# Perceiver attention reordered: K in its own layout, two heads on halves of the array, batches written out

## Chip, core and metric

The kernel runs on one core of a Trainium2 chip. The time is that of one execution on the device in microseconds (us), the median of several runs; fewer is better.

## The reference

Two layers, each a gated cross attention and a gated mixture of experts, on x of 8 x 100 x 512 with a context of 8 x 722 x 512, all fp32. The change is in the first step, a perceiver attention in which the 100 rows of x are the latents and the context gives the keys:

```
def _L0_xattn_ref(x, latents, mask, ...):        # x: context 8x722x512, latents: 8x100x512
    xn = layernorm(x, ln_x_g, ln_x_b)
    ln = layernorm(latents, ln_l_g, ln_l_b)
    q = ln @ Wq                                  # 512 -> 16 heads of 64
    kv = concatenate((xn, ln), axis=1) @ Wkv     # 822 keys a batch, 512 -> 2 x 1024
    k, v = split(kv, 2, axis=-1)
    sim = einsum('bhid,bhjd->bhij', heads(q) * 64 ** -0.5, heads(k))
    sim = where(mask_full, sim, max_neg)
    attn = softmax(sim, axis=-1)
    out = einsum('bhij,bhjd->bhid', attn, heads(v)) -> 8 x 100 x 1024
    return layernorm(out @ Wout, ln_o_g, ln_o_b)
x = x + tanh(g_xattn[0]) * _L0_xattn_ref(ctx, layernorm(x), mask, ...)
```

Behind it come the first mixture (4 experts), a strided attention and the second mixture (8 experts). They are not touched.

## The kernel before

Each step is a stage of its own with a block of instructions for each engine; the engines run in their own written order and meet at semaphores. The stage of the change is `perceiver_attention`.

At the start it loads the weights `wkv` in eight pieces and splits each in two fp32r parts, hi (a rounded copy, ScalarE) and lo (the difference, VectorE). It then works batch by batch, eight of them, in a hardware loop of seven turns and a last turn written out. A batch has 822 keys (722 context rows and 100 latents, in seven tiles of up to 128 rows) and 16 heads in eight pairs (hp = 0 to 7).

- **Normalising**: VectorE's `moments` and `normalise` in the middle of the batch before, GpSimd's `scale` (two operations a tile) behind it.
- **prepare**: TensorE transposes a normalised tile (L402) into one of the two banks of `kv_ps`, ScalarE copies hi (L281; for the latents also `lat_t`), VectorE subtracts lo (L581).
- **queries**: 32 fp32 matmuls (L411) into `s_ps`; ScalarE and VectorE write `q_hi` and `q_lo` in eight pieces each (L290, L596), each head's copy on both halves of the partitions.
- **keys(hp, part)**: K of a pair of heads in two parts of 512 and 310 columns, each four steps of three matmuls (`three`, L388 to L390: hi x hi, and the two cross terms). ScalarE copies hi of each head (64 partitions) into `k_two`, VectorE puts lo on the other 64 partitions (L305, L603), so that one matmul over 128 rows contracts q with hi and lo of k at once.
- **values(half, t)**: V of four pairs for a tile of keys, the same three terms, 12 matmuls of 512 columns (also L388 to L390), copied by ScalarE (L297). A half's seven tiles stand in one run: the first half at the start of the batch, the second behind pair 4.
- **scores(hp, x)**: for head x of the pair two passes, `q_hi` and `q_lo`, over two parts (L451, L452), into `s_ps`, which holds one head.
- **maximum** (VectorE, L613, adds the mask and keeps the row maximum), **exponent** (ScalarE, L315), **divide** (VectorE, L618 and L619).
- **transposes(hp, x)**: seven of 100 x 128 (L465) into the two banks of `t_ps`, four and three; ScalarE copies head 0 (L311), VectorE head 1 (L625), both called `move_t`.
- **attend(hp)**: 14 matmuls (L476), the two heads on halves of the output's partitions, that is of the array's columns; VectorE's `move_o` copies the result (L630).
- **finish**: the projection with `wout` (eight fp32 matmuls, L485, into the bank `w_ps`), the output's layernorm and the residual (L634 to L645).

TensorE's order in pairs 1 to 7 is, for x in 0, 1: transposes(hp-1, x), scores(hp, x), keys(hp+1, x); then attend(hp-1). The eight banks of 512 fp32 columns are: `kv_ps` 2, `s_ps` 2, `t_ps` 2, `o_ps` 1, `w_ps` 1.

## Time and profile before

| | us |
|---|---|
| median of 3 runs | 2489.97 (2474.49 to 2490.97) |
| profiled execution | 2482.1 |
| its span | 2479.9 |
| perceiver stage in it | 0 to 1,137 |

The profile is of one execution. PE is TensorE's matmul, PEld its weight loads, DVE VectorE, ACT ScalarE, POOL GpSimd. Busy times of PE overlap each other, since matmuls are pipelined and their ends are modelled: what a matmul costs is read from the distance between the starts of two that follow each other. In a timeline a bracket gives the idle time before a row and what ended it. PEclk is the clock that TensorE was granted, as a share of 2.4 GHz.

### The profile page before, as it was taken

Reading aid. Unit: us, or ns where it says so; the run is one execution under the profiler, and the core shown is the slowest. Engines: PE = TensorE matmul, PEld = TensorE weight load, DVE = VectorE, ACT = ScalarE, POOL = GpSimd, SP = SyncE. Lnnn points to the kernel's source line nnn. Section 1 sums busy time; section 2 is a strip of 40 time slices with the busy share of each in tenths; the row PEclk is TensorE's granted clock in tenths of the full one; section 3 lists DMA queues with packets and bytes.
Section 4 is the critical chain, followed back from the end, with each engine's and each line's share of the span. In section 5 each row is a group of like instructions: output and inputs, shape, how many; then the busy total and the mean of one; then the engine's idle time right before and its main releaser. Section 6 shows DMA issues by size and latency. Waiting matters only on the chain. (4 is left out here: it accounts for less than half of the span.)

```text
span 2479.9 us, 39705 instructions
## 1 busy us (share of the span) xinstructions
PE 2062.0 (83%) x12984; PEld 1706.0 (69%) x12984; DVE 1242.9 (50%) x2517; ACT 975.6 (39%) x2047; POOL 599.4 (24%) x547
## 2 busy tenths in 40 slices
PE   2899999999999999994499999999568627888783
PEld 2777878787878777772377777777466517787682
DVE  4484847576665657453333333333045354445444
ACT  2453445444444444442333333332343234444440
POOL 4030302012030303000333333331111023455443
PEclk9999999999999999996699999999786758899896
DMA  6001010100001010003533333331860164444436
GB/s 218 2 1 36 1 36 1 37 1 17 21 1 36 1 36 1 8 1 123 189 98 98 101 102 102 94 96 64 246 172 0 41 235 160 133 123 135 144 119 174
DMA packets 105987, 198.68 MB, mean 80 GB/s; under 512 B 13978, under 2 KB 14778, under 8 KB 105850
## 3 DMA queue, kind: packets, MB, share of 16 engines
q1 hardware_dynamic: 98896, 182.10, 23.1%
q0 software_dynamic: 6144, 13.13, 2.0%
q8 instruction: 85, 1.39, 0.2%
q10 hardware_dynamic: 810, 1.64, 0.2%
q14 instruction: 52, 0.43, 0.1%
HBM read 164.83 MB, written 31.98 MB: 79 GB/s over the span
## 5 line engine op out<-in xcount | busy, mean ns | idle before, releaser
L249 POOL TENSOR_TENSOR a_rows<-a_rows,a_gain_x 128x512 f32<-128x512 f32 (+1 forms) x48 | 71.2, 1484 | 803.2 <-DVE a_rows L570 803.2
L715 PE MATMUL f_banks<-f_wab_hi,f_x_hi 128*128 x448 | 189.1, 422 | 17.2 <-DVE f_wab_lo L1286 13.7
L305 ACT ACTIVATE a_k_two<-a_kv_ps 64x512 fp32r<-64x512 f32 (+1 forms) x256 | 130.1, 508 | 170.9 <-PE a_kv_ps L390 167.6
L715 PE MATMUL m_banks<-m_wab_hi,m_x_hi 128*128 x512 | 164.8, 322 | 31.2 <-DVE m_wab_lo L1286 27.8
L603 DVE TENSOR_TENSOR a_k_two<-a_kv_ps,a_k_two 64x512 fp32r<-64x512 f32 (+1 forms) x256 | 149.4, 584 | 78.3 <-ACT a_k_two L305 72.9
L388 PE MATMUL a_kv_ps<-a_wkv_hi,a_kvin_hi 128*128 128x512 f32 (+1 forms) x448 | 179.4, 401 | 9.4 <-DVE a_k_two L603 9.4
L388 PE MATMUL a_kv_ps<-a_kvin_hi,a_wkv_hi 128*128 128x512 f32 (+1 forms) x512 | 183.7, 359 | 0.6
L1316 DVE TENSOR_TENSOR f_h_sb<-f_s_sb,f_banks 128x256 f32<-128x256 f32 x112 | 47.2, 421 | 272.0 <-ACT f_s_sb L1082 272.0
L390 PE MATMUL a_kv_ps<-a_kvin_hi,a_wkv_lo 128*128 128x512 f32 (+1 forms) x512 | 179.8, 351 | 0.0
L389 PE MATMUL a_kv_ps<-a_kvin_lo,a_wkv_hi 128*128 128x512 f32 (+1 forms) x512 | 178.7, 349 | 0.0
L716 PE MATMUL f_banks<-f_wab_lo,f_x_hi 128*128 x448 | 178.6, 399 | 0.0
L717 PE MATMUL f_banks<-f_wab_hi,f_x_lo 128*128 x448 | 178.2, 398 | 0.0
L389 PE MATMUL a_kv_ps<-a_wkv_lo,a_kvin_hi 128*128 128x512 f32 (+1 forms) x448 | 177.4, 396 | 0.0
L390 PE MATMUL a_kv_ps<-a_wkv_hi,a_kvin_lo 128*128 128x512 f32 (+1 forms) x448 | 176.9, 395 | 0.0
L315 ACT ACTIVATE a_probs<-a_probs,a_neg_max 100x822 f32<-100x822 f32 x128 | 125.8, 983 | 109.3 <-DVE a_neg_max L613 108.3
L716 PE MATMUL m_banks<-m_wab_lo,m_x_hi 128*128 x512 | 153.0, 299 | 0.0
L717 PE MATMUL m_banks<-m_wab_hi,m_x_lo 128*128 x512 | 152.9, 299 | 0.0
L613 DVE CUSTOM_DVE_ANT_0 a_probs<-a_s_ps,a_mask_add 100x822 f32<-100x822 f32 x128 | 129.6, 1012 | 45.1 <-PE a_s_ps L452 42.9
L297 ACT ACTIVATE a_v_sb<-a_kv_ps 128x512 f32<-128x512 f32 (+1 forms) x112 | 66.8, 596 | 216.6 <-PE a_kv_ps L390 216.6
L1082 ACT ACTIVATE f_s_sb<-f_banks 128x256 f32<-128x256 f32 x112 | 43.0, 384 | 253.3 <-PE f_banks L717 253.3
L1016 POOL TENSOR_TENSOR f_wy_lo<-f_raw,f_wy_hi 128x512 fp32r<-128x512 f32 x64 | 83.0, 1296 | 233.8 <-ACT f_wy_hi L1060 233.8
L715 PEld LDWEIGHTS m_banks<-m_wab_hi,m_x_hi 128*128 128x128 f32 x512 | 106.3, 208 | 34.5 <-issue 34.5
(349 smaller groups left out, 5156.3 us busy)
## 6 DMA issues: line engine op xcount, KB each, us to landing
f_raw<-f_pieces SPq DMA_DIRECT2D x192, 256.0 KB, 2.7
m_raw<-m_pieces SPq DMA_DIRECT2D x192, 256.0 KB, 2.8
a_rows<-ctx SPq DMA_DIRECT2D x8, 1280.0 KB
g_rows<-ctx SPq DMA_DIRECT2D x8, 1280.0 KB, 10.0
...
```

What stands on the lines that cost most here:

```text
L249: own.link(nc.gpsimd.tensor_tensor(row, row, g[0:n, :], ALU.mult))
L305: nc.scalar.activation(k_two[halves[x], hp % 2, x, c:c + n], kv_ps[halves[x], c:c + n], ACT.Copy).then_inc(k_hi_done, 1)
L315: nc.scalar.activation(probs[0:M, x, 0:KEYS], probs[0:M, x, 0:KEYS], ACT.Exp, scale=-1.0, bias=neg_max[0:M, x:x + 1], accum_out=row_sum[0: ...
L388: nc.tensor.matmul(out, hi_l, hi_r, start=first, stop=False)
L389: nc.tensor.matmul(out, hi_l, lo_r, start=False, stop=False)
L390: return nc.tensor.matmul(out, lo_l, hi_r, start=False, stop=last)
L603: ins = nc.vector.tensor_tensor(k_two[halves[1 - x], hp % 2, x, c:c + n], kv_ps[halves[x], c:c + n], k_two[halves[x], hp % 2, x, c:c + n]. ...
L613: nc.vector.tensor_tensor_reduce(out=probs[0:M, x, 0:KEYS], in0=s_ps[0:M, 0:KEYS], in1=mask_add[0:M, :], scale=-1.0, scalar=3.0e38, op0=AL ...
L715: nc.tensor.matmul(out, left_hi, right_hi, start=start, stop=False)
L716: nc.tensor.matmul(out, left_hi, right_lo, start=False, stop=False)
L717: return nc.tensor.matmul(out, left_lo, right_hi, start=False, stop=stop)
L1016: nc.gpsimd.tensor_tensor(split_dst(wab_lo, wy_lo, c), raw[:, n % RING, :], split_dst(wab_hi, wy_hi, c).bitcast(F32), ALU.subtract).then_i ...
```

## The change

- **K**: one `k_hi` and one `k_lo` in the layout in which K leaves PSUM (two heads on 128 partitions), one copy and one subtraction a part, one buffer instead of two. `q_hi` and `q_lo` likewise, in two pieces each instead of eight.
- **Scores**: both heads in one call. `s_ps` has four banks, two for each head. Each head takes three passes (hi x hi, hi x lo, lo x hi) over its 64 partitions; the heads alternate matmul by matmul.
- **V**: two buffers (`v_sb` by half). The 14 tiles are spread over pairs 0 to 5 by FILL = 4, 3, 2, 2, 2, 1, behind the pair's other work.
- **Transposes**: one bank `t_ps`. Four tiles, copied by ScalarE, then three, copied by VectorE, for each head. The bank `w_ps` is gone: queries and projection go through `o_ps` like attend.
- **Order**: TensorE runs scores(n), attend(n-2), then the transposes of n-1 in four rounds between halves of keys(n+1), then values. The projection of a batch stands in pair 1 of the next, its layernorm in pairs 2 and 4. The latents' tile is prepared first (ORDER). All of a batch's `prepare`, the next batch's first keys and its queries stand in pair 7.
- **Start**: eight staging buffers for `wkv`; K's halves of the weights come and are split first, V's halves after the first queries.
- **Batches** are written out, eight times the code instead of a loop; bank use is counted per bank (`kv_free`, `o_free`).

The diff, cut to what the text speaks of:

```diff
-        k_two = sb("k_two", [P, 2, 2, KEYS], F32R)
-        v_sb = sb("v_sb", [P, KT, HALF])
-        q_hi = sb("q_hi", [P, PAIRS, 2, M], F32R)
-        q_lo = sb("q_lo", [P, PAIRS, 2, M], F32R)
+        k_hi = sb("k_hi", [P, KEYS], F32R)
+        k_lo = sb("k_lo", [P, KEYS], F32R)
+        v_sb = sb("v_sb", [P, 2, KT, HALF])
+        q_hi = sb("q_hi", [P, PAIRS, M], F32R)
+        q_lo = sb("q_lo", [P, PAIRS, M], F32R)
...
-        kv_ps = ps("kv_ps", [P, 2 * BANK])
-        s_ps = ps("s_ps", [P, 2 * BANK])
-        t_ps = ps("t_ps", [P, 2 * BANK])
+        stage = [wout_sb[:, :, :].rearrange("p k n -> p (k n)")[:, SW * n:SW * n + SW] for n in range(4)]
+        stage += [v_sb[:, :, :, :].rearrange("p h t n -> p (h t n)")[:, SW * n:SW * n + SW] for n in range(4)]
+
+        kv_ps = ps("kv_ps", [P, 2, BANK])
+        s_ps = ps("s_ps", [P, 2, 2 * BANK])
+        t_ps = ps("t_ps", [P, BANK])
         o_ps = ps("o_ps", [P, BANK])
-        w_ps = ps("w_ps", [P, BANK])
...
+        FILL = [4, 3, 2, 2, 2, 1, 0, 0]
...
-                if n >= STAGE:
-                    sp.wait_ge(w_lo_done, 1 + n - STAGE + 1)
-                sp.dma_start(stage[n % STAGE], wkv[P * (n // 2):P * (n // 2 + 1), SW * (n % 2):SW * (n % 2 + 1)]).then_inc(w_loaded[n % STAGE], 16)
-                if n == STAGE - 1:
-                    sp.dma_start(wq_sb[:, :, :], wq.rearrange("(k p) n -> p k n", p=P)).then_inc(pq_loaded, 16)
-            sp.wait_ge(w_lo_done, 1 + 2 * KD)
+                k, half = n % KD, n // KD
+                sp.dma_start(stage[n], wkv[P * k:P * k + P, SW * half:SW * half + SW]).then_inc(w_loaded[n], 16)
+                if n == KD - 1:
+                    sp.dma_start(wq_sb[:, :, :], wq.rearrange("(k p) n -> p k n", p=P)).then_inc(wq_loaded, 16)
...
-            def keys(i, hp, part):
-                c, n = PART[part]
-                act.wait_ge(k_ready, 1 + 2 * PAIRS * i + 2 * hp + part + 1)
-
-                act.wait_ge(s_ready, 1 + 2 * PAIRS * i + (2 * hp - 2 if hp >= 2 else 0))
-                for x in range(2):
-                    nc.scalar.activation(k_two[halves[x], hp % 2, x, c:c + n], kv_ps[halves[x], c:c + n], ACT.Copy).then_inc(k_hi_done, 1)
...
+            def keys(n, part):
+                c, w = PART[part]
+                act.wait_ge(k_ready, 2 * n + part + 1)
+                if n:
+                    act.wait_ge(s_ready, 2 * n)
+                nc.scalar.activation(k_hi[:, c:c + w], kv_bank("k", n, part)[:, 0:w], ACT.Copy).then_inc(k_hi_done, 1)
...
+                    if hp < PAIRS - 1 or i + 1 == B:
+                        if n:
+                            move_t(n - 1, 0)
+                        if hp < PAIRS - 1:
+                            keys(n + 1, 0)
+                        if n:
+                            move_t(n - 1, 1)
+                        exponent(n, 0)
+                        if hp < PAIRS - 1:
+                            keys(n + 1, 1)
...
-            def scores(i, hp, x):
-                pe.wait_ge(k_lo_done, 1 + 2 * PAIRS * i + 2 * hp + 2)
-                pe.wait_ge(q_lo_done, 1 + i + 1)
-                pe.wait_ge(max_done, 1 + 2 * PAIRS * i + 2 * hp + x)
-                for c, n in PART:
-                    k = k_two[:, hp % 2, x, c:c + n]
-                    nc.tensor.matmul(s_ps[0:M, c:c + n], q_hi[:, hp, x, :], k, start=True, stop=False)
-                    ins = nc.tensor.matmul(s_ps[0:M, c:c + n], q_lo[:, hp, x, :], k, start=False, stop=True)
-                ins.then_inc(s_ready, 1)
...
+            def scores(n):
+                i, hp = divmod(n, PAIRS)
+                if hp % QP == 0:
+                    pe.wait_ge(o_free, o_use["q", i, hp // QP] + 1)
+                wait_read(pe, ("k", n, 0), ("k", n, 1))
+                if n:
+                    pe.wait_ge(max_done, 2 * n)
+                for c, w in PART:
+                    for step, (q, k) in enumerate(((q_hi, k_hi), (q_hi, k_lo), (q_lo, k_hi))):
+                        for x in range(2):
+                            ins = nc.tensor.matmul(s_ps[0:M, x, c:c + w], q[halves[x], hp, :], k[halves[x], c:c + w],
+                                                   start=(step == 0), stop=(step == 2))
+                            if c and step == 2:
+                                ins.then_inc(s_ready, 1)
...
+            for i in range(B):
+                for hp in range(PAIRS):
+                    n = PAIRS * i + hp
+                    scores(n)
+                    if n >= 2:
+                        attend(n - 2)
+                    if hp < PAIRS - 1:
+                        if n:
+                            transposes(n - 1, 0, 0)
+                        keys(n + 1, 0, ALL[:KD // 2])
+                        if n:
+                            transposes(n - 1, 0, 1)
+                        keys(n + 1, 0, ALL[KD // 2:])
+                        if n:
+                            transposes(n - 1, 1, 0)
+                        keys(n + 1, 1, ALL)
+                        if n:
+                            transposes(n - 1, 1, 1)
+                    elif i + 1 < B:
+                        prepare(i + 1, ORDER[0])
+                        prepare(i + 1, ORDER[1])
+                        transposes(n - 1, 0, 0)
+                        prepare(i + 1, ORDER[2])
+                        transposes(n - 1, 0, 1)
+                        prepare(i + 1, ORDER[3])
+                        transposes(n - 1, 1, 0)
+                        prepare(i + 1, ORDER[4])
+                        queries(i + 1, 0)
+                        transposes(n - 1, 1, 1)
+                        prepare(i + 1, ORDER[5])
+                        prepare(i + 1, ORDER[6])
+                        keys(n + 1, 0, ALL)
+                        keys(n + 1, 1, ALL)
+                        queries(i + 1, 1)
+                    else:
+                        for x in range(2):
+                            for r in range(2):
+                                transposes(n - 1, x, r)
+                    if hp == 0 and i == 0:
+                        pe.wait_ge(w_lo_done, 2 * KD)
+                    for v in range(V_FROM[hp], V_FROM[hp] + FILL[hp]):
+                        if hp == 1 and i and v == V_FROM[hp] + 1:
+                            finish(i - 1)
+                        values(i, v)
...
+                    if n >= 2:
+                        move_o(n - 2)
+                    if hp < PAIRS - 1 or i + 1 == B:
+                        if n:
+                            move_t(n - 1, 0)
+                        maximum(n, 0)
+                        if hp < PAIRS - 1:
+                            keys(n + 1, 0)
+                        divide(n, 0)
+                        if n:
+                            move_t(n - 1, 1)
+                        maximum(n, 1)
+                        if hp < PAIRS - 1:
+                            keys(n + 1, 1)
+                        divide(n, 1)
+                    else:
...
+                    if hp == 2 and i:
+                        ins = project(i - 1)
+                        if i + 1 == B:
+                            ins.then_inc(var_done, 1)
+                    if hp == 4:
+                        wait_std()
+                        first, end = (0 if i + 1 < B else OUT), (NT + 1 if i else NT)
+                        own.link(nc.vector.reciprocal(rstd[:, first:end], std[:, first:end]))
+                        if i + 1 < B:
+                            again_latent()
+                        if i:
+                            finish(i - 1)
+                    if hp == 5 and i + 1 < B:
+                        last_latent()
+                        normalise_rows(range(0, 3))
+                    if hp == 6 and i + 1 < B:
+                        normalise_rows(range(3, CT))
...
```

## Rows read from the trace of the kernel before

**Rows 1.** The page: busy us of each engine, share of the span, instructions.

```profile
PE 2062.0 (83%) x12984; PEld 1706.0 (69%) x12984; DVE 1242.9 (50%) x2517; ACT 975.6 (39%) x2047; POOL 599.4 (24%) x547
```

**Rows 2.** Windows: the perceiver stage; PE, PEld, DVE, ACT, POOL busy, PEclk, DMA.

```profile
0.00:1137.00 1137.00, 1032.75 (x6944) 838.81 (x6944) 698.87 (x1360) 500.36 (x945) 163.50 (x123) 0.99 0.08 25
```

**Rows 3.** PE's timeline (start us, us): projections of two batches, queries between them.

```profile
596.63 0.59 PE L485 MATMUL a_w_ps<-a_wout_sb,a_out_t 128*100 128x512 f32 x1
...
722.96 0.35 PE L411 MATMUL a_s_ps<-a_lat_t,a_wq_sb 128*128 128x100 f32 x1
...
730.18 0.59 PE L485 MATMUL a_w_ps<-a_wout_sb,a_out_t 128*100 128x512 f32 x1
```

**Rows 4.** PE's timeline: attend, transposes, scores of one head.

```profile
652.95 1.42 PE L476 MATMUL a_o_ps<-a_probs_t,a_v_sb 128*64 128x100 f32 x28
654.30 0.82 PE L465 MATMUL a_t_ps<-a_ident,a_probs 100*128 100x100 f32 x7
654.90 0.45 PE L451 MATMUL a_s_ps<-a_k_two,a_q_hi 128*100 128x512 f32 x1
655.19 0.39 PE L452 MATMUL a_s_ps<-a_k_two,a_q_lo 128*100 128x512 f32 x1
655.42 0.30 PE L451 MATMUL a_s_ps<-a_k_two,a_q_hi 128*100 128x310 f32 x1
655.56 0.31 PE L452 MATMUL a_s_ps<-a_k_two,a_q_lo 128*100 128x310 f32 x1
```

**Rows 5.** PE's timeline at the edge of a batch.

```profile
716.60 0.64 PE L476 MATMUL a_o_ps<-a_probs_t,a_v_sb 128*64 128x100 f32 x9 [1.22 <-issue]
```

**Rows 6.** Groups by form, 0 to 1,140 us; then the timeline of DVE and ACT.

```profile
L603 DVE TENSOR_TENSOR a_k_two<-a_kv_ps,a_k_two 64x310 fp32r<-64x310 f32 x128 | 61.3, 479 | 3.2
...
L305 ACT ACTIVATE a_k_two<-a_kv_ps 64x310 fp32r<-64x310 f32 x128 | 54.2, 424 | 91.8 <-PE a_kv_ps L390 90.2
...
L581 DVE TENSOR_TENSOR a_kvin_lo<-a_kv_ps,a_kvin_hi 128x512 fp32r<-128x512 f32 x40 | 26.1, 682 | 1.5 <-ACT a_kvin_hi L281 1.5
...
L281 ACT ACTIVATE a_kvin_hi<-a_kv_ps 128x512 fp32r<-128x512 f32 x40 | 22.4, 598 | 22.3 <-PE a_kv_ps L402 22.3
...
656.12 1.00 DVE L613 CUSTOM_DVE_ANT_0 a_probs<-a_s_ps,a_mask_add 100x822 f32<-100x822 f32 x1
...
657.16 0.98 ACT L315 ACTIVATE a_probs<-a_probs,a_neg_max 100x822 f32<-100x822 f32 x1 [1.30 <-DVE a_neg_max L613]
...
658.27 0.16 DVE L618 RECIPROCAL a_row_inv<-a_row_sum 100x1 f32<-100x1 f32 x1 [1.14 <-ACT a_probs L315]
658.47 0.65 DVE L619 TENSOR_SCALAR a_probs<-a_probs,a_row_inv 100x822 f32<-100x822 f32 x1
...
659.03 0.95 DVE L625 COPY a_probs_t<-a_t_ps 128x400 f32<-128x400 f32 x2
```

**Rows 7.** DVE's timeline while GpSimd scales rows.

```profile
567.86 2.15 DVE L619 TENSOR_SCALAR a_probs<-a_probs,a_row_inv 100x822 f32<-100x822 f32 x1
```

**Rows 8.** Timeline: the stage's last prepare and first queries; its last write.

```profile
49.84 0.93 PE L402 MATMUL a_kv_ps<-a_ident,a_lat 100*128 100x100 f32 x4 [1.76 <-POOL a_lat L250]
...
51.80 9.54 PE L411 MATMUL a_s_ps<-a_lat_t,a_wq_sb 128*128 128x100 f32 x64 [1.03 <-issue]
...
1135.54 0.75 DVE L645 SCALAR_TENSOR_TENSOR a_tail<-a_tail,a_tanh_g,a_res 100x512 f32<-100x512 f32 x1
```

**Rows 9.** PE's timeline after two waits; the window behind the first.

```profile
71.64 0.79 PE L388 MATMUL a_kv_ps<-a_wkv_hi,a_kvin_hi 128*128 128x512 f32 x1 [5.76 <-DVE a_k_two L603]
72.23 0.63 PE L389 MATMUL a_kv_ps<-a_wkv_lo,a_kvin_hi 128*128 128x512 f32 x1
72.66 0.63 PE L390 MATMUL a_kv_ps<-a_wkv_hi,a_kvin_lo 128*128 128x512 f32 x1
...
71.60:75.60 4.00, 3.96 (x9) 3.14 (x10) 1.49 (x3) 0.00 (x0) 0.00 (x0) 0.50 0.13 18
...
1115.14 2.60 PE L476 MATMUL a_o_ps<-a_probs_t,a_v_sb 128*64 128x100 f32 x28 [1.84 <-issue]
```

732 lines of the change are left out of this document (354 added, 378 removed).

## The prediction, made before the changed kernel was run

> **What bounds the kernel now.** I read the page's busy times first, then the table of stages. Over the kernel TensorE (PE) is busy 83%; in the perceiver stage, 1,137 of 2,480 us, it is busy 1,033 us, VectorE (DVE) 699 and ScalarE (ACT) 500, at a mean granted clock of 0.99 [rows 1, 2]. The change touches this stage only, so everything after 1,137 us is taken as it is. Busy time of PE overlaps itself, so I went to its timeline and used distances between starts. One batch is the distance between two projections: 730.18 - 596.63 = 133.55 us [rows 3].
>
> What one pair of heads costs PE, start to start [rows 4]: attend 1.35 us, seven transposes 0.60, scores of one head 0.80 (0.29 + 0.23 + 0.14 + 0.14). The last two figures are what a matmul of 512 and of 310 columns costs whatever it computes. Key projection is then 12 x 0.23 + 12 x 0.145 = 4.5 us. A pair without values takes 2 x 0.80 + 2 x 0.60 + 4.5 + 1.35 = 8.7 us. A batch of 133.55 is eight pairs (69.6), 14 value tiles of 12 x 0.23 = 2.8 us (39.2), 14 of queries (7.22 [rows 3]) and projection, 3 to 4 of preparing, and the rest, about 9 us, waits at the batch's edge, of which the 1.22 us before an attend is among the longest [rows 5]. So PE's own work is about 124.5 us and its waits 9 us.
>
> **Edit 1, scores on halves of the array.** Before: per pair 2 heads x 2 passes over 822 keys, 1.60 us. After: 3 passes for each head, each on 64 of 128 rows, the two heads issued alternately. If the halves run together, a pass costs 0.23 for the 512 part; for the 310 part I take 0.165, as a weight load with its short matmul can come every 0.086 us (0.60 / 7, transposes) and there are two. Sum 3 x (0.23 + 0.165) + 0.06 for the change of form (0.29 against 0.23) = 1.25 us. Bounds: 3 x (0.23 + 0.145) = 1.13 when nothing is added, 2 x 1.13 + 0.1 = 2.36 us when the halves take turns. No row has matmuls on halves of the rows. The nearest is attend, which puts two heads on halves of the columns: 28 records in 1.35 us, 0.048 each, where a transpose of as many columns needs 0.086 in one pass; so the halves plainly overlap there. I take 1.25, a gain of 0.35 per pair.
>
> Between the bounds lies another mechanism: a load into one half waits for that half's own matmul. A pass is then matmul plus load, 3 x (0.23 + 0.086) + 3 x (0.145 + 0.086) + 0.06 = 1.7 us. The Trainium skill's page "TensorE: Matmul & The Clock Gate", in its part on packing small matmuls ("The mechanism"), says this: a load overlaps a running matmul only when the row groups differ. In the full array the trace doesn't bear that out, as scores, each with new weights, start 0.23 and 0.14 apart [rows 4]; by the rule the sum below would be 0.45 x 64 = 29 us higher. No row shows it inside a half.
>
> **Edit 2, K kept as it leaves PSUM.** Per pair ACT does two copies of 128 partitions instead of four of 64: 0.60 + 0.42. DVE does two subtractions, 0.68 + 0.48, instead of four of the same lengths [rows 6] (a column costs the same on 64 partitions and on 128). That frees DVE 1.16 us and ACT 1.02 us per pair, nothing by itself, as PE is the bound; it pays only where PE waits for k. Query copies fall from eight to two on each engine.
>
> **Edit 3, one transpose bank.** The seven transposes of a head are now 4 + 3 with a copy between, and key work in the gap hides the copy. Each group still pays the switch of about 0.07, so per pair I take 1.36 where 1.20 stood: +0.15 us. Bounds: 0 to +0.3.
>
> **Edit 4, the new order, where the waits come from.** K, scores and transposes of neighbouring pairs now form one chain through DVE. Let t = 0 be the end of scores(n) in a pair without values. PE: attend to 1.42, four transposes to 1.80, half of keys part 0 to 3.19, three transposes to 3.49, other half to 4.88, transposes to 5.26, part 1 to 7.0, transposes to 7.3. A result is ready about 0.17 after that. DVE, in its written order: move_t to 4.16 (0.46 each: 0.95 for two), maximum to 5.24 (1.01), k_lo when ACT has copied, 5.70 to 6.38, divide after the exponent. The exponent stands behind ACT's move_t (T ready 5.43, done 6.15) and takes 1.08 to 1.11: 7.23. Divide to 8.11 (0.85), move_t to 8.57, maximum(n,1) to 9.63, k_lo part 1 to 10.11 [durations: rows 6]. Only then may scores(n+1) start. PE is through at 7.3, so **a pair without values waits 2.85 us**. One value tile (2.8) just covers it, two cover it fully, so pairs 0 to 4 (4, 3, 2, 2, 2 tiles) wait nothing worth counting. Pair 5 (one tile) and pair 6 (none) also carry the next batch's normalising; GpSimd scales rows meanwhile and stretches a divide from 0.65 up to 2.15 us [rows 6, 7]. I add 1.0 to each: pair 5 waits 1.0, pair 6 waits 3.85.
>
> Pair 7 holds the batch's edge. From the end of its scores: attend 1.42, two prepares to 2.4, transposes to 2.75, prepare 2 waits for its bank (latent copies 0.9 on ACT, 0.57 on DVE) until 3.6, the second round of transposes for DVE's prepare 2 and move_t until 6.05, queries(0) 3.6 long from 6.9 to 10.5, prepares to 11.7, then keys wait until DVE has done queries, move_t, maximum(n,1) and prepare 5: 13.97. Keys to 18.5, queries(1) to 22.1. Its work is 17.8, its waits 4.3 us.
>
> Per batch, scores of 1.25 included: pair 0 19.85 (8.55 + 4 x 2.8 + 0.1), pair 1 23.4 (8.55 + 8.4 + projection 6.45), pairs 2 to 4 42.6, pair 5 12.35, pair 6 12.4, pair 7 23.35. Sum **133.95 us against 133.55**: the scores' gain is spent on the split transposes, and nine microseconds of waits are still nine, only longer and in one place.
>
> **Edit 5, start and end.** Batches written out remove loop branches that no row shows as idle; bound zero. At the start the latent tile goes first and keys need only half of the weights. Before, the last prepare is at 49.84 [rows 8], GpSimd being held up by DVE's eight weight halves; now four stand there, so I take 47.3 (45 to 50). Keys 7 us at the low clock, queries 7.2: first scores at 62.4. The first batch lacks one projection, one attend: 126.05. Then 6 x 133.95 = 803.7; the last batch to its last scores 109.85; from there to the last write 26.7 (two DVE chains 9.8, second attend at 12.65, projection 6.5, tail 5.7). Sum 1,128.7, against 1,135.54 + 0.75 = 1,136.3 [rows 8]: **-7.6 us**. The profiled execution before took 2,482.1 us (span 2,479.9), 0.3% under the median 2,489.97 of runs from 2,474.49; I count from 2,482.1.
>
> **The clock.** After 5.76 us of waiting at 65.9 us, PE starts at 71.64 with the granted clock at 0.50, the lower of its two levels (1.2 of 2.4 GHz): spacing 0.43 instead of 0.23. At the end of the stage a stretch of little work with a wait of 1.84 us is enough: attend takes 2.60 instead of 1.42, which by its length is the lower level too [rows 9]. In the middle of batches waits are about 1.2 us [rows 5], and the stage's mean clock is 0.99 [rows 2]. The 3.85 us of pair 6 lie between the two, nearer the first, and pair 7 begins with sparse work. So I expect the clock to fall there. Cost: scores +0.9 (three passes at 0.20 + 0.115 more), attend +1.2, transposes +0.5, queries(0) +1.2 (half of 9.54 - 7.22, the cost for all 64 records [rows 3, 8]): 3.8 us x 7 + 2.1 in the last batch = **+28.7 us**.
>
> **Rivals.** A, likeliest, 0.38: all as above with the falling clock: 2,482.1 - 7.6 + 28.7 = **2,503.2 us**. For it those two stretches; against it that neither is a wait of this length.
> B, 0.30: the clock holds: **2,474.5 us**, range 2,460 to 2,487.
> C, 0.17: slower because the halves of the rows don't overlap. Place: scores; price 0.45 (loads not hidden) to 1.1 us (in turn) in each of 64 pairs, +29 to +71 on B: 2,503 to **2,545 us**, and up to 2,574 if the clock falls too. It decides from 0.4 us per pair. For it: no row. Against it: attend on column halves.
> D, 0.10: faster. Waits of the edge are 2 us less per batch (-14), the split costs nothing (-10), scores take 1.13 (-8): **2,443 us**. For it only that each is a bound.
> E, 0.05: straight code or a semaphore chain that I didn't see adds 1 us per pair: 2,540.
>
> **How the numbers follow.** About 1% is what can be told from no change. Faster by over 1% (D, part of B, whose low end is there): 0.17. Within 1%: most of B, two thirds of A: 0.52. Slower: third of A, C, E: 0.31. Range: A and B whole, half of D, the lower half of C: 2,450 to 2,548; A's own is 2,490 to 2,520.
>
> **What would show it.** Scores of a pair near 1.25 us; 2.0 or more is C. PE idle ahead of the scores of pair 7 near 3.9 us, released by k_lo on DVE. Granted clock about 0.5 for some microseconds behind it; 1.00 is B. Distance of projections 134 (B) or 138 us (A). First scores near 62 us. The forecast is wrong if DVE's order doesn't bind as laid out, for instance if scores of pair 7 start within 1 us of PE's last transpose.

## The result

The changed kernel takes **2,500.4 us** (median; 2,492.2 to 2,512.4) where the kernel before, run beside it on the same chips, takes 2,479.1 (2,471.2 to 2,491.0). The ratio is 1.0084, with an interval of 1.0069 to 1.0100: slower by 0.8%, just inside what was called no change.

Busy times of the changed kernel, from its page. TensorE's are a hair up, VectorE's and ScalarE's clearly down (1,242.9 and 975.6 in [rows 1]):

```profile
PE 2073.5 (83%) x13240; PEld 1696.4 (68%) x13240; DVE 1080.8 (43%) x2343; ACT 888.5 (35%) x1867; POOL 598.8 (24%) x547
```

So 162 us of VectorE and 87 us of ScalarE were saved, and the kernel is slower. The stage as a whole and three stretches of it, in the table of windows (us, then PE, PEld, DVE, ACT, POOL busy, granted clock, DMA share, GB/s):

```profile
0.00:1160.00 1160.00, 1038.89 (x7200) 828.71 (x7200) 542.93 (x1186) 413.25 (x765) 165.58 (x123) 0.97 0.07 24
568.00:580.00 12.00, 9.33 (x84) 7.89 (x86) 8.20 (x17) 5.34 (x11) 8.15 (x6) 1.00 0.00 0
...
594.00:599.00 5.00, 4.43 (x13) 3.52 (x14) 1.65 (x4) 0.93 (x2) 0.00 (x0) 0.66 0.88 301
...
1120.00:1159.00 39.00, 25.55 (x154) 16.62 (x153) 14.37 (x32) 8.58 (x17) 0.00 (x0) 0.73 0.00 0
```

The mean clock of the stage is 0.97 where it was 0.99 [rows 2]. Steady batches and the end of the stage, from the timeline of TensorE and of VectorE:

```profile
499.34 1.02 PE L511 MATMUL a_o_ps<-a_wout_sb,a_out_t 128*100 128x512 f32 x2
...
635.53 1.02 PE L511 MATMUL a_o_ps<-a_wout_sb,a_out_t 128*100 128x512 f32 x2
...
1158.28 0.75 DVE L683 SCALAR_TENSOR_TENSOR a_tail<-a_tail,a_tanh_g,a_res 100x512 f32<-100x512 f32 x1
```

One batch is 635.53 - 499.34 = 136.19 us (133.55 in [rows 3]); four of the six steady batches are 136.2, two 137.6. The stage ends at 1,159.0 where it ended at 1,136.3 [rows 8]: +22.7 us, as much as the difference of the medians (21.3). The six steady batches hold 18.0 of it (they are 133.65 on average before, 136.65 after), the two ends 4.7. The two profiled executions differ by 27.9 us in their spans; the other 5.2 lie in the stages behind, which the change does not touch.

I added up the distances between starts on TensorE over one batch of each kernel, each distance to the kind of work that begins it, shown waits apart:

| per batch, us | before (from 596.63) | after (from 499.34) |
|---|---|---|
| scores | 12.85 | 10.58 |
| transposes | 10.09 | 8.83 |
| attend | 10.94 | 10.83 |
| keys, 512 columns | 22.85 | 25.27 |
| keys, 310 columns | 14.63 | 14.41 |
| values | 39.15 | 40.67 |
| projection, prepare, queries | 17.09 | 16.87 |
| waits shown | 5.95 | 8.73 |
| sum | 133.55 | 136.19 |

The scores do give 2.3 us and the transposes 1.3. Keys of 512 columns, values and waits take 6.7 back. About 1.5 us of the keys' time is the low clock, as shown below. So this batch has 2.8 us more of waits, 1.5 us more from the clock, and 1.6 us less of work.

The scores of one pair, changed kernel, timeline of TensorE:

```profile
526.10 0.47 PE L474 MATMUL a_s_ps<-a_k_hi,a_q_hi 64*100 64x512 f32 x2
526.41 0.39 PE L474 MATMUL a_s_ps<-a_k_lo,a_q_hi 64*100 64x512 f32 x2
526.64 0.39 PE L474 MATMUL a_s_ps<-a_k_hi,a_q_lo 64*100 64x512 f32 x2
526.88 0.30 PE L474 MATMUL a_s_ps<-a_k_hi,a_q_hi 64*100 64x310 f32 x2
527.01 0.31 PE L474 MATMUL a_s_ps<-a_k_lo,a_q_hi 64*100 64x310 f32 x2
527.15 0.31 PE L474 MATMUL a_s_ps<-a_k_hi,a_q_lo 64*100 64x310 f32 x2
527.40 1.42 PE L502 MATMUL a_o_ps<-a_probs_t,a_v_sb 128*64 128x100 f32 x28
```

Each row is two matmuls (x2), one per head, and the rows are 0.31, 0.23, 0.24, 0.13, 0.14 and 0.25 us apart (the last distance is to attend): two heads take the time of one, 1.30 us in all.

The waits of one batch, the same view: a value tile of pair 4, the scores that begin pairs 6 and 7, three inside pair 7, and keys behind the last:

```profile
552.69 0.50 PE L408 MATMUL a_kv_ps<-a_wkv_hi,a_kvin_hi 128*128 128x512 f32 x1 [0.89 <-DVE a_k_lo L639]
...
568.29 0.48 PE L474 MATMUL a_s_ps<-a_k_hi,a_q_hi 64*100 64x512 f32 x2 [1.17 <-DVE a_k_lo L639]
...
579.43 0.48 PE L474 MATMUL a_s_ps<-a_k_hi,a_q_hi 64*100 64x512 f32 x2 [2.37 <-DVE a_k_lo L639]
...
584.34 0.63 PE L426 MATMUL a_kv_ps<-a_ident,a_rows 128*128 128x128 f32 x4 [0.90 <-DVE a_kvin_lo L623]
...
586.85 0.54 PE L488 MATMUL a_t_ps<-a_ident,a_probs 100*128 100x100 f32 x4 [1.18 <-DVE a_probs_t L659]
...
594.57 0.47 PE L408 MATMUL a_kv_ps<-a_kvin_hi,a_wkv_hi 128*128 128x512 f32 x1 [2.22 <-DVE a_kvin_lo L623]
...
595.58 0.61 PE L409 MATMUL a_kv_ps<-a_kvin_lo,a_wkv_hi 128*128 128x512 f32 x1
595.99 0.63 PE L410 MATMUL a_kv_ps<-a_kvin_hi,a_wkv_lo 128*128 128x512 f32 x1
```

All six have VectorE behind them, which is busy 47% of the stage (542.93 of 1,160). Its share says nothing; its order does. The last rows show the clock: one microsecond after the wait of 2.22 the matmuls stand 0.42 us apart instead of 0.23, the lower level of 1.2 GHz, until 598.97. That is the window with 0.66.

### The profile page after: what moved, and what is told of

Read it like the earlier page. It is cut to its first block and busy times, and to the rows that moved or that the text cites. A ratio compares the mean times of both kernels' runs of the same rounds, so it can differ in the third digit from the quotient of the medians.

```text
span 2507.8 us, 37895 instructions
## 1 busy us (share of the span) xinstructions
PE 2073.5 (83%) x13240; PEld 1696.4 (68%) x13240; DVE 1080.8 (43%) x2343; ACT 888.5 (35%) x1867; POOL 598.8 (24%) x547
## 5 line engine op out<-in xcount | busy, mean ns | idle before, releaser
L408 PE MATMUL a_kv_ps<-a_kvin_hi,a_wkv_hi 128*128 128x512 f32 (+1 forms) x512 | 200.0, 391 | 15.5 <-DVE a_kvin_lo L623 15.5
L282 POOL TENSOR_TENSOR a_lat<-a_lat,a_gain_l 100x512 f32<-100x512 f32 x8 | 20.2, 2522 | 776.7 <-DVE a_lat L607 776.7
L408 PE MATMUL a_kv_ps<-a_wkv_hi,a_kvin_hi 128*128 128x512 f32 (+1 forms) x448 | 184.7, 412 | 9.5 <-DVE a_k_lo L639 9.5
L409 PE MATMUL a_kv_ps<-a_kvin_lo,a_wkv_hi 128*128 128x512 f32 (+1 forms) x512 | 185.4, 362 | 0.0
L410 PE MATMUL a_kv_ps<-a_kvin_hi,a_wkv_lo 128*128 128x512 f32 (+1 forms) x512 | 185.1, 362 | 0.0
L342 ACT ACTIVATE a_probs<-a_probs,a_neg_max 100x822 f32<-100x822 f32 x128 | 125.9, 984 | 107.6 <-DVE a_neg_max L646 107.5
L488 PE MATMUL a_t_ps<-a_ident,a_probs 100*128 100x100 f32 x896 | 124.2, 255 | 12.0 <-DVE a_probs_t L659 9.6
L331 ACT ACTIVATE a_k_hi<-a_kv_ps 128x512 fp32r<-128x512 f32 (+1 forms) x128 | 65.5, 511 | 193.3 <-PE a_kv_ps L410 187.5
L488 PEld LDWEIGHTS a_t_ps<-a_ident,a_probs 100*128 100x128 f32 x896 | 99.9, 142 | 37.7 <-issue 11.9
```

What stands on the lines that cost most here:

```text
L331: nc.scalar.activation(k_hi[:, c:c + w], kv_bank("k", n, part)[:, 0:w], ACT.Copy).then_inc(k_hi_done, 1)
L342: nc.scalar.activation(probs[0:M, x, 0:KEYS], probs[0:M, x, 0:KEYS], ACT.Exp, scale=-1.0, bias=neg_max[0:M, x:x + 1], accum_out=row_sum[0: ...
L408: nc.tensor.matmul(out, hi_l, hi_r, start=first, stop=False)
L409: nc.tensor.matmul(out, hi_l, lo_r, start=False, stop=False)
L410: return nc.tensor.matmul(out, lo_l, hi_r, start=False, stop=last)
L488: ins = nc.tensor.transpose(t_ps[:, M * (t - a):M * (t - a) + M], probs[0:M, x, P * t:P * t + P], ident[0:M, 0:M])
```

## Experiments

Every ratio is to the kernel before, run on the same chip; the changed kernel stands at 1.0084. A difference to the changed kernel in us is between medians of different chips, on which the kernel before took 2,475.0 to 2,479.1 us, so it is good to about 4 us.

### Do the halves of the array run side by side? (in_turn)

```diff
-for c, w in PART:
-    for step, (q, k) in enumerate(...):
-        for x in range(2):
+for x in range(2):
+    for c, w in PART:
+        for step, (q, k) in enumerate(...):
```

> The changed kernel with one edit: the six matmuls of head 0 are issued before the six of head 1, instead of alternately; same work, same waits. Theory O (the halves of the array run side by side when their matmuls alternate, 1.31 us per pair in the changed kernel): a pair's scores become 6 x 0.23 + 6 x 0.145 + 0.06 = 2.3 us, 1.0 us more in each of 64 pairs; pairs 5 and 6 of a batch, which wait for VectorE anyway, may swallow a part: 50 to 64 us slower than the changed kernel, so 2,550 to 2,564 us. Theory S (the 1.31 us are just six short passes, the halves don't overlap): scores stay at 1.31 us and the time within 5 us of 2,500.

Measured: 2,551.8 us, ratio 1.0294 (1.0271 to 1.0316), 51 us slower than the changed kernel. The scores of one pair, timeline of TensorE:

```profile
545.74 0.47 PE L474 MATMUL a_s_ps<-a_k_hi,a_q_hi 64*100 64x512 f32 x1
546.05 0.39 PE L474 MATMUL a_s_ps<-a_k_lo,a_q_hi 64*100 64x512 f32 x1
546.29 0.39 PE L474 MATMUL a_s_ps<-a_k_hi,a_q_lo 64*100 64x512 f32 x1
546.29 0.52 PE L474 MATMUL a_s_ps<-a_k_hi,a_q_hi 64*100 64x512 f32 x2
...
547.57 0.31 PE L502 MATMUL a_o_ps<-a_probs_t,a_v_sb 128*64 128x100 f32 x2
```

From 545.74 to 547.57 it is 1.83 us against 1.30: the order costs 0.53 us per pair, not the 1.0 expected. Even written in turn the heads overlap: the rows of x2 hold head 0's 310 columns and head 1's 512, and the first of them starts at 546.29 together with head 0's third matmul. The page "TensorE: Matmul & The Clock Gate" of the Trainium skill, in "The mechanism", says that TensorE looks past running matmuls for loads into another row group; these rows agree.

The steady batches take 143.2 to 143.6 us, 6.8 more on average. In one of 143.2, 7.0 us longer than the batch from 499.34, 4.3 are those 0.53 x 8, 1.3 are longer waits, and the rest is the low clock, which there lay on scores, attend and prepare of pair 7 (3 us) while the keys ran at the full one (-1.5). In four of the six it lay on the keys as well (25.3 us). One reason for the longer waits is a row of VectorE in pair 6:

```profile
599.52 1.53 DVE L652 TENSOR_SCALAR a_probs<-a_probs,a_row_inv 100x822 f32<-100x822 f32 x1
```

This divide lies beside GpSimd's scaling and takes 1.53 us instead of 0.65. So the stretching that the prediction counted on does occur, where the two happen to meet. Theory O holds, but with half its price per pair: that 51 us lies in the expected 50 to 64 is luck, since waits and clock add what the scores do not cost.

### What the low clock costs (fill_pe, fill_both)

```diff
 prepare(i + 1, ORDER[6])
+pe.wait_ge(max_done, 2 * n + 1)
+for j in range(6):
+    nc.tensor.matmul(s_ps[:, 0, 0:BANK], wkv_hi[:, j % KD, 0:P], kvin_lo[:, j % KD, 0:BANK], ...)
 keys(n + 1, 0, ALL)
```

> The changed kernel with six extra matmuls of 512 columns (6 x 0.23 = 1.4 us, their result is never used) in pair 7, where TensorE waits 2.2 us for kvin_lo ahead of the keys of the next batch. Theory K (the granted clock falls behind that wait, and the low clock costs 1.6 us of the 25.3 us of keys): the clock stays at 1.00, keys fall back, 7 x 1.6 = 11 us less: about 2,489 us. Rival (the longer keys come from something else, or the clock falls all the same): within 3 us of 2,500.

Measured: 2,489.9 us, ratio 1.0052 (1.0034 to 1.0070). Table of windows around the same keys:

```profile
586.00:600.00 14.00, 13.22 (x97) 11.86 (x98) 5.69 (x12) 4.03 (x9) 0.00 (x0) 1.00 0.37 121
```

The keys run at full clock: 23.8 us per batch instead of 25.3. But only one of the six steady batches got down to 134.65; in others attend, scores or prepare of pair 7 now took 1 to 1.5 us more, so that they stand at 136.0 to 136.2. The low clock had moved to the other wait. The six together are 4.6 us shorter, the stage 7.5. The total is the 2,489 us expected, but part of the keys' gain was lost again in pair 7, and 2.9 us came from the start and the end of the stage. The next run fills the other wait too:

```diff
+if hp == PAIRS - 1:
+    pe.wait_ge(max_done, 2 * n - 1)
+    (six such matmuls)
 scores(n)
```

> The kernel fill_pe with six more extra matmuls of 512 columns (1.4 us) where TensorE waits 2.4 us ahead of the scores of pair 7 (their result is never used). Theory K (the granted clock falls when TensorE stands still near these two waits; in fill_pe it still fell around scores and attend of pair 7 in some batches, 0.5 to 1.5 us each): it holds through every batch, all steady batches take 134.6 us and none 136: 4 to 8 us less than fill_pe, about 2,484 us. Rival (it falls by some other rule, or the extra matmuls cost what they save): the same as fill_pe within 3 us.

Measured: 2,484.4 us, ratio 1.0037 (1.0015 to 1.0058). Five of six steady batches take 134.5 to 134.7; in the sixth queries(0) ran at the low clock (9.56 against 7.19). Twelve matmuls without use, about 3.3 us of work per batch, made the kernel 16 us faster by the medians and 12 by the ratios. Those five batches are 2.0 us shorter than the changed kernel's average. In the changed kernel the low clock costs 1.5 us in four batches (keys) and 3.0 in two (scores and attend as well), which is 2.0 on average; the added matmuls cost about what they take from the waits. Filling the two waits of 2.2 and 2.4 us keeps the clock up in most batches. More the traces don't settle: in the batch from 499.34 it stayed at 1.00 behind the 2.37 us and fell behind the 2.22 us; in two others it fell at both; and it fell in one batch of this run, where the longest wait was 1.3 us.

### The two waits that were not forecast (no_root)

Ahead of an exponent of pair 5, changed kernel, timeline of ScalarE (pair 4 has the same):

```profile
562.53 0.50 ACT L338 ACTIVATE a_probs_t<-a_t_ps 128x400 f32<-128x400 f32 x1
563.05 1.28 ACT L342 ACT_TABLE_LOAD   x1
564.34 0.98 ACT L342 ACTIVATE a_probs<-a_probs,a_neg_max 100x822 f32<-100x822 f32 x1
```

The square roots (deviations, L303) in pairs 3 and 4 need another table than the exponent, and the load stands in the chain.

```diff
-nc.scalar.activation(std, var, ACT.Sqrt, bias=eps)
+nc.scalar.activation(std, var, ACT.Identity if dev[0] > 2 else ACT.Sqrt, bias=eps)
```

> The changed kernel with the square roots inside the loop over batches replaced by a copy with the same bias, so that the standard deviations are variances there (this part of the computation is changed); ScalarE then has no table to load for them nor again for the exponent behind them. Theory L (the waits of 0.89 us in pair 4 and 1.17 us ahead of the scores of pair 6 come from the two table loads of 1.28 us before an exponent): both waits go, 2.0 x 7 = 14 us less: about 2,486 us. Theory G (of the forecast: GpSimd's scaling stretches VectorE's divide in these pairs): within 4 us of 2,500.

This kernel leaves out the square roots in the loop, so its values are others. The whole time, 3,105 us, is of no use: the later stages route tokens by the values, which is the likely reason why they take longer, though no run shows it. They lie behind 1,137.6 us. The stage itself can be read: it ends at 1,137.6 instead of 1,159.0, and between 540 and 590 us the timeline of TensorE shows these waits and no other:

```profile
567.72 0.48 PE L474 MATMUL a_s_ps<-a_k_hi,a_q_hi 64*100 64x512 f32 x2 [2.35 <-DVE a_k_lo L639]
573.90 0.63 PE L426 MATMUL a_kv_ps<-a_ident,a_rows 128*128 128x128 f32 x4 [0.57 <-DVE a_kvin_lo L623]
576.41 0.54 PE L488 MATMUL a_t_ps<-a_ident,a_probs 100*128 100x100 f32 x4 [1.19 <-DVE a_probs_t L659]
584.14 0.47 PE L408 MATMUL a_kv_ps<-a_kvin_hi,a_wkv_hi 128*128 128x512 f32 x1 [2.22 <-DVE a_kvin_lo L623]
```

The waits of 0.89 and 1.17 us are gone, the 2.35 of pair 6 stands. Batches are 133.7 to 135.4 (mean 134.35 against 136.65), the stage is 21 us shorter, more than the 14 expected: the six steady batches hold 13.8 of it, what stands before and behind them 7.6. Theory L holds; GpSimd had no part in these two. The page "ScalarE: Activation LUTs" of the Trainium skill, in "What ACT_TABLE_LOAD costs", gives a drain of 1.38 us on top of the load. Here the load starts 0.02 us after the end of the copy ahead of it and the exponent 0.01 us after the load; no drain shows.

### Where V's tiles lie (grouped)

```diff
-FILL = [4, 3, 2, 2, 2, 1, 0, 0]
+FILL = [5, 2, 0, 0, 7, 0, 0, 0]
```

> The changed kernel with V's 14 tiles in three pairs instead of six: FILL = 5, 2, 0, 0, 7, 0, 0, 0 instead of 4, 3, 2, 2, 2, 1, 0, 0. Theory W (in the changed kernel the chain through VectorE ends about 2.4 us after TensorE's own work of a pair without values, and a value tile covers it): pairs 2, 3, 5 and 6 each wait 2.3 us ahead of the next scores, 9.2 us where pairs 4 to 6 wait 4.4 now; fewer changes between keys and values save about 1; the granted clock may fall once more per batch, 0 to 3 us: 4 to 7 us per batch, 2,528 to 2,550 us. Rival (the waits belong to pairs 5 and 6 with their normalising, not to pairs without values): 0 to 10 us slower than the changed kernel.

Measured: 2,588.9 us, ratio 1.0454 (1.0412 to 1.0496). Timeline of TensorE, one batch:

```profile
701.83 0.48 PE L474 MATMUL a_s_ps<-a_k_hi,a_q_hi 64*100 64x512 f32 x2 [2.31 <-DVE a_k_lo L639]
714.53 0.48 PE L474 MATMUL a_s_ps<-a_k_hi,a_q_hi 64*100 64x512 f32 x2 [2.46 <-DVE a_k_lo L639]
...
757.76 0.75 PE L474 MATMUL a_s_ps<-a_k_hi,a_q_hi 64*100 64x512 f32 x2 [3.69 <-DVE a_k_lo L639]
...
771.50 0.47 PE L474 MATMUL a_s_ps<-a_k_hi,a_q_hi 64*100 64x512 f32 x2 [2.28 <-DVE a_k_lo L639]
```

Every pair without values now waits 2.3 us or more (2.26 to 3.74 over the six steady batches): this is the price of the new chain, and the spreading of V over six pairs is what hides it. The loss of 88 us is larger than the 28 to 50 expected. One wait is 3.69 because it has the table load in it. Together the waits are 7.2 us more in this batch; and with more waits above 2 us the clock falls more often (attend 14.0 us per batch instead of 10.8, transposes 10.1 instead of 8.8, scores 11.9 instead of 10.6). The price of the clock was underrated, and the table load in that wait was not in the expectation.

### Edits 1 and 2 undone in the new order (two_pass, half_copies2)

```diff
-k_hi = sb("k_hi", [P, KEYS], F32R); k_lo = ...
+k_two = sb("k_two", [P, 2, KEYS], F32R)
 # keys: ScalarE and VectorE, four copies of 64 partitions each per pair
 # scores: per head q_hi, then q_lo, against k_two[:, x, :] on 128 rows
```

> The changed kernel with edits 1 and 2 undone inside the new order: K is again kept per head as its high half and its low half one above the other (four copies of 64 partitions on ScalarE, four subtractions on VectorE per pair, eight query copies on each), and each head's scores are two passes over the whole array; FILL, the order of all queues, one transpose bank stay (the mask is kept in bfloat16, exact, to make room). Theory P (edits 1 and 2 pay in this order by shortening the chain that ends at k_lo): scores 1.60 + 0.06 us instead of 1.31 (+0.3 x 8), the waits ahead of the scores of pairs 6 and 7 longer by a k_lo of 0.48 and copies behind it, about 1.5 us each, query copies in pair 7 +1: about 6 us per batch, 45 us in all: 2,540 to 2,550 us. Rival (the copies are hidden, only the passes count): 2.4 x 8 = 19 us, about 2,520 us.

Measured: 2,666.5 us, ratio 1.0773 (1.0744 to 1.0802), 166 us slower than the changed kernel; 45 were expected. Timeline of TensorE, waits in pair 4, ahead of the scores of pair 6, and in pair 7:

```profile
789.89 0.50 PE L411 MATMUL a_kv_ps<-a_wkv_hi,a_kvin_hi 128*128 128x512 f32 x1 [2.38 <-DVE a_k_two L644]
...
807.02 0.45 PE L476 MATMUL a_s_ps<-a_k_two,a_q_hi 128*100 128x512 f32 x1 [2.52 <-DVE a_k_two L644]
...
841.46 0.77 PE L411 MATMUL a_kv_ps<-a_kvin_hi,a_wkv_hi 128*128 128x512 f32 x1 [5.75 <-DVE a_kvin_lo L624]
```

A steady batch takes 157.0 to 160.4. In the one of 157.0 waits are 22.4 us instead of 8.7, scores work 14.3 instead of 10.6 (1.58 us per pair where the clock is high). The 13.7 us of added waits lie in four places: a second value tile waits for the bank that the second part of K holds (+4.3: 0.9 to 2.4 us in pairs 0 and 2 to 4, nothing or 0.9 before), the scores of pairs 6 and 7 wait for k_lo (+2.7), the eight query copies stand ahead of the last prepares (5.75 us, +3.5), and an attend waits 3.1 us for the last of them. To tell K's copies from the queries':

```diff
-nc.scalar.activation(k_hi[:, c:c + w], kv_bank(...)[:, 0:w], ACT.Copy)
+for x in range(2):
+    nc.scalar.activation(k_hi[halves[x], c:c + w], kv_bank(...)[halves[x], 0:w], ACT.Copy)
 # the same for k_lo on VectorE
```

> The changed kernel with one thing undone: the copies of K, k_hi on ScalarE and k_lo on VectorE, are made in two halves of 64 partitions each (four and four instructions per pair instead of two and two). Layout, scores, query copies and all orders stay, and the result is the same. It splits what two_pass undid together (166 us slower than the changed kernel, 20.8 us per steady batch, of which 3.7 in scores, 13.7 in waits). Theory P (it is the number of K copies in the chain of VectorE and ScalarE): the waits for k_lo grow as in two_pass, those of value tiles by 4.3 and those of scores by 2.7 us per batch, and the clock costs about 2 more: 9 x 7 = 63 us, about 2,563 us. Rival (the query copies at the batch's edge are the larger part of two_pass's loss, 3.5 us of keys and 3.1 us of attend waiting there): less than 35 us slower than the changed kernel.

Measured: 2,580.7 us, ratio 1.0421 (1.0397 to 1.0445), 80 us slower than the changed kernel. The waits behind k_lo are 10.9 us per batch instead of 4.4, those for kvin_lo and probs_t unchanged (4.3). The value tiles' own distances grow too, 43.1 us instead of 40.7. One row of VectorE's timeline shows the term:

```profile
759.42 1.39 DVE L641 TENSOR_TENSOR a_k_lo<-a_kv_ps,a_k_hi 64x512 fp32r<-64x512 f32 x2 [0.64 <-ACT a_k_hi L332]
```

1.39 us where one instruction over 128 partitions takes 0.69. Theory P holds, with 80 us instead of 63: the added waits (6.5 us per batch) are as expected, the longer distances of the value tiles (2.4) were not in the sum. K's copies are half of two_pass's loss, and the query copies, the passes and the clock the other half.

### Taking the chain out (two_probs, late_wait, spread, all_three)

The chain in the changed kernel, pair 6, timeline of VectorE; scores ended at 569.68:

```profile
573.32 0.47 DVE L659 COPY a_probs_t<-a_t_ps 128x300 f32<-128x300 f32 x1 [1.00 <-PE a_t_ps L488]
573.71 1.01 DVE L646 CUSTOM_DVE_ANT_0 a_probs<-a_s_ps,a_mask_add 100x822 f32<-100x822 f32 x1
...
575.38 0.69 DVE L639 TENSOR_TENSOR a_k_lo<-a_kv_ps,a_k_hi 128x512 fp32r<-128x512 f32 x1 [0.66 <-ACT a_k_hi L331]
...
576.93 0.70 DVE L652 TENSOR_SCALAR a_probs<-a_probs,a_row_inv 100x822 f32<-100x822 f32 x1
577.55 0.46 DVE L659 COPY a_probs_t<-a_t_ps 128x300 f32<-128x300 f32 x1
577.93 1.00 DVE L646 CUSTOM_DVE_ANT_0 a_probs<-a_s_ps,a_mask_add 100x822 f32<-100x822 f32 x1
...
578.86 0.47 DVE L639 TENSOR_TENSOR a_k_lo<-a_kv_ps,a_k_hi 128x310 fp32r<-128x310 f32 x1
```

The maximum starts 4.03 us after its scores were there. It writes to probs, which must first be transposed for the pair before. A second set of probs takes that away; the same edit changes the orders of VectorE and ScalarE to use it, so that the run does not tell the buffer from the order:

```diff
-probs = sb("probs", [P, 2, KT * P])
+probs = sb("probs", [P, 4, KT * P])          # set 2 * (n % 2) + x
-if n:      dve.wait_ge(t_ready, 4 * (n - 1) + 2 * x + 2)
+if n >= 2: dve.wait_ge(t_ready, 4 * (n - 2) + 2 * x + 2)
 # VectorE: maximum 0, 1; move_o; normalise; divide 0; move_t; divide 1; keys 0, 1; move_t
```

> The changed kernel with two sets of probs (even and odd pairs; the mask is kept in bfloat16, exact for 0 and -2^100, to make room), and VectorE's and ScalarE's orders set to use it: both maxima stand right behind the scores, exponents next, then the moves and divisions. Theory W (a pair without values waits because maximum(n, x) has to wait for the transposes of pair n-1 on the same probs): the chain from the scores' end to the last k_lo falls from 10.1 to about 8.4 us, the waits of pairs 5 and 6 (1.2 + 2.4) fall below 1, the wait in pair 7 from 2.2 to about 0.9, and the clock holds: (3.0 + 1.3 + 1.6) x 7 = 41 us less, about 2,459 us. Rival (VectorE's or ScalarE's sheer work sets these waits, whatever its order): no more than 10 us less.

Measured: 2,462.3 us, ratio 0.9936 (0.9914 to 0.9958), 38 us faster than the changed kernel; a batch takes 132.3. What is left in pairs 5, 6 and 7, on TensorE:

```profile
549.99 0.54 PE L488 MATMUL a_t_ps<-a_ident,a_probs 100*128 100x100 f32 x4 [1.32 <-DVE a_probs_t L659]
563.19 0.54 PE L488 MATMUL a_t_ps<-a_ident,a_probs 100*128 100x100 f32 x4 [1.67 <-DVE a_probs_t L659]
566.56 0.47 PE L474 MATMUL a_s_ps<-a_k_hi,a_q_hi 64*100 64x512 f32 x2 [0.82 <-issue]
```

Theory W holds only in part. Pair 4 no longer waits, the waits inside pair 7 fall from 4.30 to 2.55 us, and in all six steady batches the clock stays up (keys of 512 columns 24.0 instead of 25.3). But pairs 5 and 6 wait as long as before, 1.32 and 1.67 + 0.82 against 1.17 and 2.37, where the theory had less than 1. In pair 6 the scores end at 556.51 and the last k_lo at 566.46, a chain of 9.95 us and not 8.4. Two rows of VectorE in it:

```profile
561.19 1.48 DVE L652 TENSOR_SCALAR a_probs<-a_probs,a_row_inv 100x822 f32<-100x822 f32 x1
...
565.98 0.48 DVE L639 TENSOR_TENSOR a_k_lo<-a_kv_ps,a_k_hi 128x310 fp32r<-128x310 f32 x1 [1.13 <-ACT a_k_hi L331]
```

The maxima now start right behind the scores, but 2.43 us of normalising stand ahead of the divisions, which take 1.48 and 1.09 us beside GpSimd's scaling where 0.65 is usual. So the wait for the buffer was replaced by a wait for this work. A batch is 4.3 us shorter on average, not 5.9; that the total came out near the 41 us expected is luck, as start and end of the stage gave another 11 us.

Then one edit after another. First the wait of scores for k_lo by parts:

```diff
-wait_read(pe, ("k", n, 0), ("k", n, 1))
 for part, (c, w) in enumerate(PART):
+    wait_read(pe, ("k", n, part))
```

> The kernel two_probs with one more edit: scores wait for the first 512 columns of k_lo before their first matmul, and for the other 310 only before the matmuls that read them. Theory W (the 0.8 us that the scores of pair 7 still wait in two_probs are k_lo's second part alone): 0.8 x 7 = 5 us less than two_probs, about 2,457 us; rival (they wait for the maxima or the first part as well): the same as two_probs, 2,462 us.

Measured: 2,457.8 us, ratio 0.9923 (0.9895 to 0.9952); 131.6 per batch. The 0.8 us are gone; by the ratios alone the difference could not be told, by the batches it can. Then VectorE's normalising and the table:

```diff
-if hp == 5: last_latent(); normalise_rows(range(0, 3))      # ahead of divide
-if hp == 6: normalise_rows(range(3, CT))
+if hp == 4: last_latent()                                   # behind the last move_t
+if hp in (4, 5, 6): normalise_rows(range(2 * hp - 8, 2 * hp - 6))
 # ScalarE: the second deviations(LAT, NT) ahead of pair 4's exponent, not behind it
```

> The kernel late_wait with two more edits: VectorE normalises the next batch's rows two tiles at a time at the end of pairs 4, 5 and 6 instead of three at a time ahead of the divisions of pairs 5 and 6; the square root for the latents stands directly behind the one for the rows, so that ScalarE changes its table once per batch and not twice. Theory W (in two_probs the transposes of pairs 5 and 6 wait 1.32 and 1.67 us for a move_t that stands behind 2.4 us of normalising on VectorE): these 3.0 us per batch go, 21 us less than late_wait, about 2,436 us. Rival (VectorE's work in pair 6 is too much whatever its order, and the wait moves to k_lo): less than 8 us.

Measured: 2,440.5 us, ratio 0.9861 (0.9835 to 0.9887); 128.65 in five of the six steady batches, 2.95 less. The two waits of 3.0 us are gone; a prepare waits 0.44 us longer and the keys of 512 columns take 0.34 less. (In the sixth batch, 130.15, queries ran at the low clock, with no wait above 1.51 us.) These are two edits in one, and which of them gave how much was not told apart. Last the queries of pair 7 ahead of its keys:

> The kernel spread with one more edit: in pair 7 the second half of the queries is computed before the keys of the next batch, not after them, on all queues. Theory E (the 1.3 us that keys wait for kvin_lo in two_probs are covered by the 3.6 us of queries, and what then waits is the copying of keys ahead of scores, of which the split wait leaves about 0.4 us): 0.9 x 7 = 6 us less than spread, about 2,430 us. Rival (what the queries covered before comes back in full as a wait ahead of the scores, 1.2 us): the same as spread.

Measured: **2,435.0 us, ratio 0.9835 (0.9809 to 0.9861)**, faster than both kernels. A batch takes 128.1 us, its waits are 2.2 us in all, the longest this one:

```profile
684.95 0.63 PE L426 MATMUL a_kv_ps<-a_ident,a_rows 128*128 128x128 f32 x4 [1.51 <-DVE a_kvin_lo L623]
```

Is the cover of the values still needed once the chain fits? all_grouped is all_three with the FILL of grouped.

> The kernel all_three with the same FILL = 5, 2, 0, 0, 7, 0, 0, 0. Theory W (with two sets of probs the chain fits into a pair without values): no new waits, and three groups of values instead of six save about 0.25 us each: 5 us less than all_three, about 2,430 us. Rival (VectorE's work per pair leaves no room once nothing covers it): 0.5 us or more in each of four pairs, 2,449 us or more.

Measured: 2,490.0 us, ratio 1.0058 (1.0035 to 1.0081), 55 us slower than all_three. Timeline of TensorE, pairs 3 and 4:

```profile
659.83 0.48 PE L488 MATMUL a_t_ps<-a_ident,a_probs 100*128 100x100 f32 x3 [1.60 <-ACT a_probs_t L338]
...
672.80 0.76 PE L488 MATMUL a_t_ps<-a_ident,a_probs 100*128 100x100 f32 x3 [4.00 <-ACT a_probs_t L338]
```

The time is in the rival's range, but the waits lie in two pairs and not in four, and neither expectation named them. Pairs 2, 5 and 6 no longer wait, but ahead of the maxima of pair 4 VectorE has 4.3 us of other work in a row (again_latent and the tail of the last batch, 665.9 to 670.3), ahead of those of pair 3 the moments (2.8 us), and ScalarE's move_t stands behind the exponent that needs the maximum. Two waits of 5.6 us together and the clock (keys of 512 at 25.3 us again, transposes at 10.0 instead of 9.0) are most of the 8.75 us by which this batch is longer. So in the faster kernel the values are still needed, to cover this work.

## Why the prediction came out as it did

The time was predicted at 2,503, with its likeliest case at 2,503.2, and is 2,500.4; the stage was to end at 1,128.7 + 28.7 = 1,157.4 and ends at 1,159.0. The time is right more exactly than its terms: that it came within 3 us is luck, since misses cancel. What the prediction had right is the mechanism that decides: a chain through VectorE that ends last in pairs without values, released by k_lo, and a low clock behind the longest waits.

- **The waits of before.** "Nine microseconds of waits are still nine" does not hold. The prediction's own terms leave 7.3 us for waits (133.55 - 69.6 - 39.2 - 14 - 3.5), not 9, and the trace shows 5.95 in that batch. The changed kernel has 8.73. So the waits grew by 2.8 us, and TensorE's work, put at 124.5 for the kernel before, was 127.6. The forecast of the changed kernel did not suffer, since its waits were added up anew; its account of where the scores' gain goes did.
- **Scores, edit 1.** 1.25 us predicted, 1.30 measured. The case in which the halves don't overlap is out, and so is the rule by which a load inside a half waits for that half's matmul (1.7 us): the passes stand 0.23 apart, as in the full array [rows 4]. in_turn shows that the alternation is worth 0.53 us per pair, 51 us in all with what hangs on it.
- **K as it leaves PSUM, edit 2.** "Nothing by itself, as PE is the bound; it pays only where PE waits for k." The second half was right, but no number was put to it. The lighter copies were in the chain's durations, so that the sum did not suffer. half_copies2 puts 80 us on K's copies alone, in the changed order. A link of the chain that ends last is not hidden work.
- **Split transposes, edit 3.** Predicted +0.15 per pair. Measured per batch: transposes -1.3, keys of 512 columns +0.9 where the clock holds, keys of 310 -0.2, together about -0.5 where +1.2 was counted. So the scores' gain was not spent here. The error of about 1.7 us in the good direction is matched by one that was not thought of: **value tiles** in six groups instead of two cost 40.7 instead of 39.2 us.
- **The chain, edit 4.** From the end of scores: maximum over at 5.24, first k_lo 5.70 to 6.38, last k_lo over at 10.11 predicted; 5.04, 5.70 to 6.39 and 9.65 measured. The form was right, and the wait of a plain pair was to be 2.85 us and is 2.37 (2.26 to 2.47 in grouped). Pair 7 was forecast at 4.3 us of waits and has 0.90 + 1.18 + 2.22 = 4.30.
- **What was added to pairs 5 and 6.** One microsecond each was put down to GpSimd stretching a divide. In the changed kernel the divides of pair 6 take at most 0.70 us and one of pair 5 takes 0.88; the two engines hardly met. In its place stands another term, in pairs 4 and 5: the table load of 1.28 us, which gives 0.89 and 1.17 us of wait (no_root). The same loads are in the trace of before (one at 559.28, ahead of an exponent); the prediction has no term for them. Sum of waits forecast 9.15, measured 8.73.
- **The clock.** The mechanism was right and its size and place were not: predicted 3.8 us per batch behind the wait of pair 6, measured 1.5 behind the wait ahead of the next batch's keys (25.3 against 23.8 us of keys), and 3.0 in the two batches of six in which it fell behind pair 6 as well (137.6 instead of 136.2). The wait of pair 6 was 2.4 us and not 3.85, and the clock mostly outlived it.
- **Steady batches and ends.** Steady 137.75 predicted, 136.65 measured on average: 6.6 us less over six. First scores at 63.4, not 62.4, and the first steady batch begins about 2 us late. From the last steady projection to the end 107.5 were predicted, the clock's share included, 113.6 measured (1,159.0 - 1,045.45): the stretch of 1,120 to 1,159 runs at 0.73, and its three attends (2.38, 2.60 and 2.60 us instead of 1.42) and its projection (8.69 instead of 7.03) take 5.0 us more than at full clock, where 2.1 had been counted for all of it. So the gain of 7.6 us at start and end did not appear; the two ends together are 4.7 us longer than before.

Why is it slower, then, with 162 us less work on VectorE? The new order makes one chain per pair out of transposes, maximum, exponent and k_lo, and it needs 9.65 us behind the scores where TensorE has 7.4 us of work. The chain is what costs; the lighter copies (two_pass, 166 us, the passes included) and the spread values (grouped, 88 us) are what makes it bearable. The steps from two_probs to all_three show it: the same scores, K and V, with waits taken out of the chain by one more buffer and other orders of the queues, and the kernel is 0.6 to 1.65% faster than before. How much of the chain comes from the order, from the one K buffer and from the one transpose bank was not told apart.

What stays open: no kernel had the old order with the new scores, and none had the second set of probs without the new orders of VectorE and ScalarE. And when exactly the clock falls is not settled; only that filling the two waits of 2.2 to 2.4 us prevents it in most batches.
